# The rows of maxima transposed at unit 26 of a stage, right behind a weighing, in place of unit 24, between two weighings

## Chip, cores and metric

One core of one Trainium2 chip runs the whole program. The metric is the device time of one execution in microseconds; the program before takes 2254.86 us (median of 3 runs, 2253.78 to 2256.43).

## What is computed

16 images of 128 channels and 1024 tokens go through multi-head attention and then through a mixture of experts. Cut to what matters here:

```python
q, k, v = (einsum('btc,hcd->bhtd', xs, W) for W in (Wq, Wk, Wv))     # 8 heads of size 16
att = softmax(einsum('bhtd,bhsd->bhts', q, k) / 4, axis=-1)           # 1024 x 1024 for each head
out = einsum('bhts,bhsd->bhtd', att, v)
x = x + (out.transpose(0, 2, 1, 3).reshape(B, T, -1) @ Wproj + bproj)
t = tokens(x); t = t + top2_mixture_of_experts(layernorm(t))          # 16 experts, hidden 512
```

The softmax subtracts each row's maximum before the exponential. The change is in the attention phase, in the way those maxima reach the second product.

## The kernel before

**Stages and units.** Heads are done in two groups (G = 2) of four, and the 1024 queries in two halves, so an image has 4 stages; a stage has UNITS = 32 units, one for each of 8 blocks of keys and 4 heads. An image has SLOTS = 128 units, numbered u = 0 to 127 below; "unit 90" of image 7 is unit 26 of its stage 2. The order is written out by hand: on every engine a Python function `batch` runs over the 128 units and emits what belongs to each, so each engine's instructions stand in one fixed order and wait for each other by semaphores.

**What a unit does.** TensorE issues one maxima matmul (`max_unit`, L1531), which runs LEAD = 45 units ahead, and one score matmul (`score_unit`, L1555). VectorE takes the row maximum of the first (`take_max`, L1009); four banks of PSUM (MRING = 4) lie between them, so that TensorE is at most four ahead. ScalarE takes the exponential of the second (`exp_unit`, L848). After every fourth unit or so TensorE weighs values with four finished exponentials (`weigh`, L1572; its four matmuls stand as x8 in the profile); within a stage this is behind units 2, 7, 10, 14, 18, 22, 26 and 30. 

**Front banks.** Scores, projections and all transposes share three banks (FRONT = 3), which go round in the order of issue; the fourth of such results must wait until ScalarE has emptied the bank of the first. `FRONT_BANK` follows this order from `front_order`, where "m" stands at unit MSLOT of a stage.

**The rows of maxima.** At unit 19 of a stage VectorE has all maxima of the next stage, and it splits them into two parts by unit 21. At unit MSLOT TensorE transposes them (`rows_of_maxima`, L1541, four matmuls), ScalarE copies the result to `m_row` (`copy_m`, L882), and two DMAs on SP's queue (`load_m`, L414, 8 KB) put them beside the queries in `arena_b`. The first score of the next stage waits for these DMAs (`m_loaded`). The transposes behind unit 24 of stage s = 0, 1, 2, 3 belong to stage s + 1, or to stage 0 of the next image.

**SP's queue** is in order too. In each image it holds, among others, the moves of stacked queries and keys for a later stage (`stack`, L405, 12 DMAs of 64 KB each for a group and a layer). The last three moves of two such sets stand right behind a `load_m`:

```python
stack(b, 1, 1, every[:9], at + 15)
load_m(b, 1)
stack(b, 1, 1, every[9:], at + 26)
...
stack(b + 1, 0, 1, every[:9], at + 78)
load_m(b, 3)
if not last:
    stack(b + 1, 0, 1, every[9:], at + 90)
```

The first set is waited for by the maxima matmul that stands at unit 35 (`stacked[1][1]`, maximum number 80), the second by the one at unit 99 (`stacked[0][1]` of the next image, number 144 = 99 + 45).

Of the kernel before, what the change touches and what calls it, by code (L numbers as in the profile page):

```python
# [25 lines left out]
UNITS = TB * HG  # L26
SLOTS = STAGES * UNITS
LEAD = 45
MSLOT = 24
FRONT, MRING = 3, 4  # L30
PRING = 16
NORMS = 14
# [70 lines left out]
def front_order():  # L103
# [5 lines left out]
    for b in range(B):  # L109
        for u in range(SLOTS):  # L110
# [5 lines left out]
            if b > 0:  # L116
# [4 lines left out]
                if u == COUNT_AT:  # L121
                    yield "counts", b - 1, 0
            if u % UNITS == MSLOT and not (b == B - 1 and u > 96):
                yield ("m", b, u // UNITS + 1) if u // UNITS + 1 < STAGES else ("m", b + 1, 0)
# [11 lines left out]
def metaformer(nc, x, wq, wk, wv, wproj, bproj, wgate, w1, w2, out):  # L136
    ctx = ExitStack()
    with ctx:
# [703 lines left out]
        def _(act):  # L842
# [34 lines left out]
            def copy_m(b, s):  # L877

                k = STAGES * b + s
                wait(act, m_psum, k + 1)  # L880
                wait(act, m_loaded, 16 * SIDES * k)
                nc.scalar.activation(m_row[0:MROWS, :], front("m", *divmod(k, STAGES))[0:MROWS, :], ACT.Copy).then_inc(m_copied, 1)  # L882
# [18 lines left out]
            def copy_rows(b, half):  # L901
                wait(act, rows_normed, TB * (b + 1))
                wait(act, scattered, 256 * b)
                js = slice(4 * half, 4 * half + 4)
                nc.scalar.activation(rows[:, 1, js, 0:C], rows[:, 0, js, 0:C], ACT.Copy).then_inc(rows_copied, 1)
# [14 lines left out]
            def batch(b, first, last):  # L920
                for u in range(SLOTS):
# [8 lines left out]
                    if not first:  # L930
# [8 lines left out]
                        if u in ROWS_AT:  # L939
                            copy_rows(b - 1, ROWS_AT.index(u))  # L940
                    if u % UNITS == MSLOT and not (last and u > 96):
                        copy_m(b, u // UNITS + 1)
# [542 lines left out]
        def _(pe):  # L1485
# [50 lines left out]
            def rows_of_maxima(b, s):  # L1536
                k = STAGES * b + s
                to = take_front("m", *divmod(k, STAGES), m_copied, k + 1)
                wait(pe, m_split, 2 * (k + 1))
                for t in range(4):  # L1540
                    last = nc.tensor.transpose(to[0:MROWS, t * P:(t + 1) * P],  # L1541
                                               m_parts_f[:, t, :, :, :].rearrange("p s a l -> p (s a l)"), ident[:, :])
                last.then_inc(m_psum, 1)
# [58 lines left out]
            def count_tokens(b):  # L1602

                w = 3 * E
                to = take_front("counts", b, 0, cs_taken, b + 1)
                wait(pe, masks_ready, b + 1)
                nc.tensor.matmul(to[:, 0:TB * w], tri_b[:, :], masks_b[:, :, :], start=True, stop=False)
                for d in range(1, TB):
                    nc.tensor.matmul(to[:, d * w:TB * w], ones_b[:, :], masks_b[:, 0:TB - d, :], start=False,
                                     stop=(d == TB - 1))  # L1610
                for j in range(TB):
                    last = nc.tensor.matmul(to[:, TB * w:(TB + 1) * w], ones_b[:, :], masks_b[:, j, :],
                                            start=(j == 0), stop=(j == TB - 1))
                last.then_inc(cs_psum, 1)
# [18 lines left out]
            def batch(b, first, last):  # L1633
                for u in range(SLOTS):
# [15 lines left out]
                    if not first:  # L1650
# [6 lines left out]
                        if u == COUNT_AT:  # L1657
                            count_tokens(b - 1)
                    if u % UNITS == MSLOT and not (last and u > 96):
                        rows_of_maxima(b, u // UNITS + 1)  # L1660
# [110 lines left out]
```

## Time and profile before

| what | value |
|---|---|
| median of 3 runs | 2254.86 us |
| the profiled execution: its time, its span | 2254.34 us, 2252.5 us |
| TensorE matmuls busy | 2106.4 us (94%) |
| VectorE busy | 1841.2 us (82%) |
| ScalarE busy | 1528.6 us (68%) |
| one image in the steady part of the attention phase | about 100.8 us (units of 0.79 us) |
| first and last transposes of the rows of maxima | 56.34 us and 1635.82 us |

The attention phase lasts until about 1660 us, then the experts follow. Time outside the span (2254.34 less 2252.5, 1.8 us) is start and end of the program. An idle time in brackets in a row of the timeline stands for the engine just before the row's first instruction, with what ended it. A row merges equal instructions that follow each other closely; its length reaches from the first start to the last end. Matmuls are pipelined, so what counts is the distance between starts.

### The profile page before, as it was taken

The page shows a single profiled execution, that of the slowest core. Times are in us where ns is not written, and L with a number is a line of the kernel's source. Part 1 is how long each engine was busy: PE and PEld are TensorE (multiplying, and loading weights), DVE is VectorE, ACT ScalarE, POOL GpSimd, SP SyncE. Part 2 cuts the span into 40 slices and gives each one's busy share as a digit, 9 for nine tenths or more (in the row PEclk, how much of TensorE's full clock was granted, in tenths as well). Part 3 has the DMA queues.
Part 4 walks back from the last instruction along what each step waited for, and adds up shares of the span by engine and source line. Part 5 has one row for each costly group of instructions (what it writes and reads, how often), then busy time and mean ns, then how long its engine had stood idle before and what let it go on. Part 6 is the DMA issues. An engine that isn't in the chain of part 4 may idle for free. (4 is left out here: it accounts for less than half of the span.)

```text
span 2252.5 us, 53329 instructions
## 1 busy us (share of the span) xinstructions
PE 2106.4 (94%) x16914; PEld 1175.1 (52%) x16914; DVE 1841.2 (82%) x4370; ACT 1528.6 (68%) x3169; POOL 1048.7 (47%) x1650
## 2 busy tenths in 40 slices
PE   5999999999999999999999999999969999899996
PEld 2333333334333333334333333333339999899996
DVE  6899999999999999999999999999925445345664
ACT  1777777777777777777777777777646566466552
POOL 3204454454445455454445455444246577455542
PEclk7999999999999999999999999999989999999997
DMA  5223323132323323232323323223162223222586
GB/s 127 48 44 63 60 58 76 36 71 45 69 53 72 61 53 74 37 70 51 67 52 68 71 43 74 39 60 57 40 190 70 71 71 86 78 71 71 159 253 178
DMA packets 135695, 171.09 MB, mean 76 GB/s; under 512 B 31568, under 2 KB 101592, under 8 KB 135414
## 3 DMA queue, kind: packets, MB, share of 16 engines
q1 hardware_dynamic: 118582, 134.25, 27.9%
q0 software_dynamic: 16896, 34.12, 4.3%
q8 instruction: 115, 1.88, 0.3%
q14 instruction: 102, 0.84, 0.1%
HBM read 64.86 MB, written 48.87 MB: 50 GB/s over the span
## 5 line engine op out<-in xcount | busy, mean ns | idle before, releaser
L1009 DVE TENSOR_REDUCE sb_m_red<-banks 128x1 f32<-128x512 f32 x2048 | 1318.8, 678 | 85.6 <-PE banks L1531 79.7
L848 ACT ACTIVATE sb_arena_a<-banks 128x512 f32<-128x512 f32 x2048 | 1088.7, 600 | 329.4 <-PE banks L1555 325.7
L1555 PE MATMUL banks<-sb_arena_b 64*128 64x512 f32 x2048 | 788.7, 460 | 21.5 <-DVE sb_res L1068 9.6
L1531 PE MATMUL banks<-sb_arena_b 62*128 62x512 f32 x2048 | 741.9, 448 | 40.4 <-DVE sb_m_red L1009 27.4
L1531 PEld LDWEIGHTS banks<-sb_arena_b 62*128 62x128 f32 x2048 | 340.7, 188 | 571.7 <-DVE sb_m_red L1009 468.5
L1572 PE MATMUL banks<-sb_arena_a,sb_arena_d 128*32 128x512 f32 x4096 | 546.0, 605 | 11.0 <-DVE sb_o_t L1041 9.3
L777 POOL DMA_INDIRECT sorted_rows<-sb_rows,sb_place x256 | 250.8, 980 | 343.3 <-PE banks L1555 325.4
L1555 PEld LDWEIGHTS banks<-sb_arena_b 64*128 64x128 f32 x2048 | 331.6, 185 | 139.5 <-ACT sb_arena_a L848 95.5
L821 POOL DMA_INDIRECT expert_out<-sb_arena_d x272 | 271.6, 999 | 242.6 <-DVE sb_arena_d L1401 178.1
L1685 PE MATMUL banks<-sb_arena_d,sb_arena_c 128*128 128x128 f32 x2176 | 290.4, 277 | 1.2 <-ACT sb_arena_d L954 0.7
L1694 PE MATMUL banks<-sb_arena_c 128*128 128x128 f32 x2176 | 289.0, 276 | 0.0
L1394 DVE COPY sb_arena_c<-sb_arena_b 128x512 f32 x272 | 134.9, 496 | 168.3 <-PE banks L1694 163.4
L1685 PEld LDWEIGHTS banks<-sb_arena_d,sb_arena_c 128*128 128x128 f32 x2176 | 267.1, 193 | 1.8 <-ACT sb_arena_d L954 1.8
L1694 PEld LDWEIGHTS banks<-sb_arena_c 128*128 128x128 f32 x2176 | 266.5, 193 | 0.0
L961 ACT ACTIVATE sb_arena_c<-banks 128x512 f32<-128x512 f32 x272 | 162.4, 597 | 113.8 <-PE banks L1685 112.2
L1391 DVE COPY sb_arena_c<-sb_arena_a 128x512 f32 x272 | 116.6, 429 | 80.2 <-issue 46.6
L968 ACT ACTIVATE sb_arena_d<-banks,sb_arena_d 128x128 f32<-128x128 f32 x272 | 99.9, 367 | 99.2 <-PE banks L1694 92.8
L1572 PEld LDWEIGHTS banks<-sb_arena_a,sb_arena_d 128*32 128x32 f32 x4096 | 80.6, 108 | 154.1 <-issue 93.8
L657 POOL TENSOR_SCALAR sb_arena_d<-sb_v_st 128x512 f32<-128x512 f32 x32 | 19.6, 614 | 269.0 <-ACT sb_v_st L873 207.7
L954 ACT ACTIVATE sb_arena_d<-banks 128x128 f32<-128x128 f32 x272 | 73.4, 270 | 35.7 <-PE banks L1677 35.2
L1677 PE MATMUL banks<-sb_ident,sb_arena_d 128*128 128x128 f32 x272 | 74.8, 276 | 19.3 <-DMA sb_arena_d<-sorted_rows 19.3
L1510 PE MATMUL banks<-sb_xt,sb_wq_r 128*128 128x512 f32 x128 | 74.2, 667 | 7.9 <-POOL sb_xt L639 7.7
(167 smaller groups left out, 1597.4 us busy)
## 6 DMA issues: line engine op xcount, KB each, us to landing
sb_arena_b<-sb_arena_c SPq DMA_DIRECT2D x768, 64.0 KB, 2.3
sb_arena_d<-sorted_rows SPq DMA_DIRECT2D x272, 66.0 KB
sb_x_in<-in_x_dram SPq DMA_DIRECT2D x16, 512.0 KB, 3.9
sb_res<-in_x_dram SPq DMA_DIRECT2D x16, 512.0 KB, 3.6
sb_x_all<-sb_res SPq DMA_DIRECT2D x16, 512.0 KB, 3.1
expert_out<-sb_arena_d POOLq DMA_INDIRECT x272
sorted_rows<-sb_rows,sb_place POOLq DMA_INDIRECT x256
sb_arena_a<-in_L_ffn_w_dram SPq DMA_DIRECT2D x4, 1024.0 KB, 7.4
```

The source lines that it names most:

```text
L777: nc.gpsimd.indirect_dma_start(out=sorted_rows[:, :], out_offset=bass.IndirectOffsetOnAxis(ap=place[:, k, j:j + 1], axis=0), in_=rows[:, k ...
L821: nc.gpsimd.indirect_dma_start(out=expert_out[:, :], out_offset=bass.IndirectOffsetOnAxis(ap=blk_dest[:, s % WR:s % WR + 1], axis=0), in_= ...
L848: nc.scalar.activation(probs[:, u % PRING, :], front("score", b, u), ACT.Exp, scale=SCALE).then_inc(exp_done, 1)
L961: nc.scalar.activation(hid[:, s % 2, :], ps_h[:, s % 2, :], ACT.Relu).then_inc(hid_done, 1)
L1009: nc.vector.tensor_reduce(out=m_red[:, s % 2, at:at + 1], in_=ps_max[:, m % MRING, :], axis=AX.X, op=ALU.max).then_inc(max_taken, 1)
L1391: nc.vector.tensor_copy(w1_blk[:, s % WR, :], w1_all[:, bass.ds(e, 1), :].rearrange("p a h -> p (a h)")).then_inc(w1_copied, 1)
L1394: nc.vector.tensor_copy(w2_blk[:, s % WR, :], w2_all[:, bass.ds(e, 1), :, :].rearrange("p a c d -> p (a c d)")).then_inc(w2_copied, 1)
L1531: nc.tensor.matmul(ps_max[:, m % MRING, :], qs[rows_of, g, l, half * HALF + t * P:half * HALF + (t + 1) * P], ks[rows_of, g, l, kh * HALF: ...
L1555: nc.tensor.matmul(to, ks[rows_of, g, l, i * P:(i + 1) * P], qs[rows_of, g, l, half * HALF:(half + 1) * HALF], start=True, stop=True).then ...
L1572: last = nc.tensor.matmul(ps_pv[32 * h:32 * h + 32, :], v_pad[:, i, HG * g + h, :], probs[:, (4 * n + h) % PRING, :], start=(i == 0), stop ...
L1685: last = nc.tensor.matmul(ps_h[:, s % 2, c * P:(c + 1) * P], w1_blk[:, s % WR, c * P:(c + 1) * P], blk_xt[:, s % 2, :], start=True, stop=True)
L1694: last = nc.tensor.matmul(ps_o[s % WR], hid[:, s % 2, c * P:(c + 1) * P], w2_blk[:, s % WR, c * P:(c + 1) * P], start=(c == 0), stop=(c == ...
```

## The change

One constant. `front_order` and the `batch` functions of TensorE and ScalarE read it; VectorE, GpSimd and SP keep their order.

```diff
-MSLOT = 24
+MSLOT = 26
```

On TensorE the four transposes (L1541) stood behind the score of unit 24, in the midst of the four units between the weighing behind unit 22 and that behind unit 26. This is the place in stage 1 of an image; before:

```order
L1572 MATMUL banks<-sb_arena_a,sb_arena_d 32x512 x4
L1531 MATMUL banks<-sb_arena_b 128x512
L1555 MATMUL banks<-sb_arena_b 128x512
L1531 MATMUL banks<-sb_arena_b 128x512
L1555 MATMUL banks<-sb_arena_b 128x512
L1541 MATMUL banks<-sb_ident,sb_m_parts 8x128 x4
L1531 MATMUL banks<-sb_arena_b 128x512
L1555 MATMUL banks<-sb_arena_b 128x512
L1531 MATMUL banks<-sb_arena_b 128x512
L1555 MATMUL banks<-sb_arena_b 128x512
L1572 MATMUL banks<-sb_arena_a,sb_arena_d 32x512 x4
L1531 MATMUL banks<-sb_arena_b 128x512
```

The same stretch of TensorE's program in the changed kernel:

```order
L1572 MATMUL banks<-sb_arena_a,sb_arena_d 32x512 x4
L1531 MATMUL banks<-sb_arena_b 128x512
L1555 MATMUL banks<-sb_arena_b 128x512
L1531 MATMUL banks<-sb_arena_b 128x512
L1555 MATMUL banks<-sb_arena_b 128x512
L1531 MATMUL banks<-sb_arena_b 128x512
L1555 MATMUL banks<-sb_arena_b 128x512
L1531 MATMUL banks<-sb_arena_b 128x512
L1555 MATMUL banks<-sb_arena_b 128x512
L1572 MATMUL banks<-sb_arena_a,sb_arena_d 32x512 x4
L1541 MATMUL banks<-sb_ident,sb_m_parts 8x128 x4
L1531 MATMUL banks<-sb_arena_b 128x512
```

The transposes have moved past two units and one weighing; everything else keeps its place.

On ScalarE the copy (L882) moves past two exponentials (L848). Before, in the same stage:

```order
L848 ACTIVATE sb_arena_a<-banks 128x512 x8
L882 ACTIVATE sb_m_row<-banks 8x512
L848 ACTIVATE sb_arena_a<-banks 128x512 x6
L873 ACTIVATE sb_v_st<-banks 128x512
```

And in the changed kernel:

```order
L848 ACTIVATE sb_arena_a<-banks 128x512 x10
L882 ACTIVATE sb_m_row<-banks 8x512
L848 ACTIVATE sb_arena_a<-banks 128x512 x4
L873 ACTIVATE sb_v_st<-banks 128x512
```

SP's queue is the same in both. This is its stretch from the moves between stages 1 and 2 to the end of an image; the three moves (L405 x3) stand between two loads of rows of maxima (L414):

```order
L405 DMA sb_arena_b<-sb_arena_c 16x1024 x21
L414 DMA sb_arena_b<-sb_m_row 2x2x512 x2
L405 DMA sb_arena_b<-sb_arena_c 16x1024 x3
L414 DMA sb_arena_b<-sb_m_row 2x2x512 x2
L405 DMA sb_arena_b<-sb_arena_c 16x1024 x12
```

Since nothing in it moves, the three moves follow the load in front of them, whenever its copy is done.

## Rows read from the trace of the kernel before

**Rows 1.** Busy time of each engine, mean over nine windows of 102 us
```profile
sum 918.00, PE 874.98 PEld 354.43 DVE 874.97 ACT 692.75 POOL 422.92; mean PE 97.22 PEld 39.38 DVE 97.22 ACT 76.97 POOL 46.99
```

**Rows 2.** Timeline of TensorE, image 7, units 87 to 99
```profile
831.07 1.07 PE L1572 MATMUL banks<-sb_arena_a,sb_arena_d 128*32 128x512 f32 x8
...
832.73 0.60 PE L1541 MATMUL banks<-sb_ident,sb_m_parts 128*8 128x128 f32 x4
...
834.20 1.06 PE L1572 MATMUL banks<-sb_arena_a,sb_arena_d 128*32 128x512 f32 x8
835.20 0.50 PE L1531 MATMUL banks<-sb_arena_b 62*128 62x512 f32 x1
...
836.41 0.49 PE L1555 MATMUL banks<-sb_arena_b 64*128 64x512 f32 x1
836.83 1.06 PE L1572 MATMUL banks<-sb_arena_a,sb_arena_d 128*32 128x512 f32 x8
...
838.17 0.63 PE L1531 MATMUL banks<-sb_arena_b 62*128 62x512 f32 x2
...
839.05 0.50 PE L1555 MATMUL banks<-sb_arena_b 64*128 64x512 f32 x1
839.48 1.06 PE L1572 MATMUL banks<-sb_arena_a,sb_arena_d 128*32 128x512 f32 x8
840.47 0.49 PE L1531 MATMUL banks<-sb_arena_b 62*128 62x512 f32 x1
```

**Rows 3.** Timeline of ScalarE, the same stretch
```profile
832.63 1.09 ACT L848 ACTIVATE sb_arena_a<-banks 128x512 f32<-128x512 f32 x2 [0.57 <-PE banks L1555]
833.60 0.57 ACT L882 ACTIVATE sb_m_row<-banks 8x512 f32<-8x512 f32 x1
...
835.76 2.07 ACT L848 ACTIVATE sb_arena_a<-banks 128x512 f32<-128x512 f32 x4 [0.64 <-PE banks L1555]
838.40 2.06 ACT L848 ACTIVATE sb_arena_a<-banks 128x512 f32<-128x512 f32 x4 [0.57 <-PE banks L1555]
```

**Rows 4.** Timeline of VectorE, the same stretch
```profile
835.73 5.12 DVE L1009 TENSOR_REDUCE sb_m_red<-banks 128x1 f32<-128x512 f32 x8 [0.64 <-PE banks L1531]
841.00 1.29 DVE L1009 TENSOR_REDUCE sb_m_red<-banks 128x1 f32<-128x512 f32 x2 [0.16 <-PE banks L1531]
```

**Rows 5.** Timeline of SP's queue, the same stretch
```profile
834.20 1.36 SPq L414 DMA_DIRECT2D sb_arena_b<-sb_m_row  x2
835.66 1.84 SPq L405 DMA_DIRECT2D sb_arena_b<-sb_arena_c  x3
```

**Rows 6.** Timeline of TensorE, ScalarE: a projection behind a weighing, unit 62
```profile
813.06 1.06 PE L1517 MATMUL banks<-sb_wv_sb,sb_xt 128*32 128x128 f32 x32
...
814.19 0.60 ACT L873 ACTIVATE sb_v_st<-banks 128x512 f32<-128x512 f32 x1 [1.02 <-PE banks L1517]
```

**Rows 7.** Timeline around unit 32 of image 10: ScalarE, SP, TensorE
```profile
1084.49 0.57 ACT L882 ACTIVATE sb_m_row<-banks 8x512 f32<-8x512 f32 x1
...
1087.32 1.36 SPq L414 DMA_DIRECT2D sb_arena_b<-sb_m_row  x2
...
1090.01 0.50 PE L1555 MATMUL banks<-sb_arena_b 64*128 64x512 f32 x2 [0.52 <-DMA sb_arena_b<-sb_m_row]
```

**Rows 8.** DMA issues: size in KB, median us from issue to landing
```profile
sb_arena_b<-sb_arena_c SPq DMA_DIRECT2D x768, 64.0 KB, 2.3
```

**Rows 9.** Timeline around unit 0 of image 7: ScalarE, TensorE
```profile
759.85 1.58 ACT L848 ACTIVATE sb_arena_a<-banks 128x512 f32<-128x512 f32 x3 [0.57 <-PE banks L1555]
...
761.09 0.50 PE L1555 MATMUL banks<-sb_arena_b 64*128 64x512 f32 x1
```

**Rows 10.** Timeline around unit 32 of image 2: ScalarE, SP, TensorE
```profile
278.47 0.57 ACT L882 ACTIVATE sb_m_row<-banks 8x512 f32<-8x512 f32 x1
...
280.47 1.47 SPq L414 DMA_DIRECT2D sb_arena_b<-sb_m_row  x2
...
283.99 0.50 PE L1555 MATMUL banks<-sb_arena_b 64*128 64x512 f32 x2 [0.54 <-DMA sb_arena_b<-sb_m_row]
```

## The prediction

> **What bounds the kernel now.** I read the busy times of the attention phase first, then the timeline of one image unit by unit on TensorE, ScalarE, VectorE and SP's queue. Over nine windows of 102 us TensorE and VectorE are both busy for 97.22 us [rows 1]: neither hides behind the other, and they take turns. The turns show in the idle times of VectorE. In the stretch of units 87 to 99 it runs dry twice, 0.64 us before 835.73 and 0.16 us before 841.00, each time until TensorE's first maxima matmul behind a weighing [rows 4]. There TensorE decides, and a delay of TensorE goes straight into the time.
>
> TensorE's own pace between two weighings is set by ScalarE and the three front banks. From 834.20 to 836.83 and on to 839.48 a group of four units and a weighing takes 2.63 and 2.65 us [rows 2]. The first unit of a group starts at 835.20, its exponential at 835.76 and lasts about 0.60 [rows 3]; the fourth score needs its bank and starts at 836.41, 0.05 behind the exponential's end at 836.36; the weighing follows 0.42 later and takes 1.00 until the next unit [rows 2]. With the transposes in its midst the group from 831.07 to 834.20 takes 3.13 us: in the old place they cost 0.50.
>
> Second, the chain behind the transposes: transposes 832.73 [rows 2], copy 833.60 to 834.17 [rows 3], the two loads from 834.20, three moves of stacked rows from 835.66 to 837.50 [rows 5]. How long the loads take to be seen is read where TensorE waits for them, in image 10: issued at 1087.32, the score starts at 1090.01, 2.69 later [rows 7]. In the stretch of rows 2 this would be 836.89, and the score of unit 96 starts at 838.17, so there is 1.28 us of slack. The third move has one move's length of 0.54 (an estimate: 1.84 for three, less 0.65 from start to start twice) and starts at 836.96; with 2.3 to land [rows 8] it is there at 839.26, and the maxima matmul of unit 99, which needs it, starts at 840.47 [rows 2]: 1.21 us of slack. The change spends both.
>
> **The change part by part.** Nothing is added or removed: 63 times four transposes of 0.60 us, a copy of 0.57 and the waits of two DMAs move; on SP's queue, what stands behind those DMAs moves with them.
>
> *The new place.* Units 89 and 90 lose the transposes ahead of them. The score of unit 90 needs the bank of unit 87, whose exponential starts at 832.63 and ends at 833.23 [rows 3]; so the score starts at 833.28, the weighing at 833.70, and the transposes at 834.70. That is 1.97 later than now.
>
> *The copy.* The trace has a case of work with a front bank right behind a weighing, the projection of unit 62: it ends at 814.12 and its copy starts at 814.19 [rows 6], since ScalarE has caught up during the weighing. So the copy starts 0.67 behind the start of the transposes, where it now starts 0.87 behind: 835.37, end 835.94, against 834.17 now. The load chain is 1.77 later, not 1.97.
>
> *TensorE behind it.* The transposes hold TensorE for 0.53; unit 91 starts at 835.23. Its exponential comes behind the copy, 0.48 after the copy's start (833.60, next start 834.08 by the pitch of four exponentials in 2.06 us [rows 3]), so 835.85 to 836.45; unit 94's score at 836.50, the weighing at 836.92 instead of 836.83. The group costs 0.09 more than in the old place. Where VectorE is behind (stage 1, whose choosing of experts keeps it busy), this shows only at unit 67. I count 0.09 for 16 stages of that kind: **1.4 us**.
>
> *The first score of the next stage.* Stage 2 to 3: natural start 838.26, loads seen at 835.94 + 0.03 + 2.69 = 838.66, so TensorE stands still for 0.40. It is nearly absorbed: the score of unit 98 has to wait for the exponential of unit 95, and starts at 839.05, although TensorE could be there at about 838.65 (838.17 and two steps of 0.24: two maxima matmuls in 0.63, one of them 0.40 long) [rows 2]. The same for stage 3 to stage 0 of the next image, but there a transpose of x stands behind unit 1 and uses up that reserve: unit 2's score starts at 761.09 [rows 9], and the exponential of unit 0, late by 0.49, pushes it. Unit 31's score starts 0.56 ahead of the first exponential at 759.85 [rows 9], unit 0's 0.34 behind that, at 759.63; with the 0.49 it is 760.12, its exponential runs from 760.68 to 761.28 (now it starts at 760.34), and unit 2's score starts at 761.33, 0.24 late. VectorE is dry at unit 3 there, so this counts: 15 images by 0.24 = **3.6 us**. Bounds: 0.09 each if all is absorbed (1.4 us), 0.49 each if nothing is (7.4 us).
>
> *Stage 0 to 1.* Here SP decides already: in image 10 the copy ends at 1085.06, yet the load is issued at 1087.32, behind nine moves, and TensorE waits for it [rows 7]. A copy 1.77 later ends at 1086.83: still in time. In image 2 the copy ends at 279.04 and the load is issued at 280.47 [rows 10]; with the new copy it is 280.84, 0.37 late. Eight images (1 to 6, 8, 9) are like image 2. There the landing is slow (3.52 from issue to score [rows 10] against 2.69), which may mean that the DMA queue decides and not the issue: 0 to 0.37 each, I take half: **1.5 us**. What is queued behind, three moves, has over 1 us of slack.
>
> *The moves behind the load of stage 3.* The largest term. SP waits for the copy with the three moves for the next image behind it. Load at 835.97, third move 2.76 later at 838.73, landing 841.03. TensorE would be at unit 99 at 840.47 + 0.09 = 840.56; it now starts at about 841.07, 0.60 later than before. VectorE is dry at that point (idle until 841.00 [rows 4]) and then has the four steps of dividing in units 100 to 103, so it decides what follows and carries the 0.60 along. 15 images by 0.60 = **9.0 us**. Bounds: 0.16 less each if VectorE's present idle time covers that much (6.6), and 1.77 - 1.21 + the 0.40 of unit 96 if the two waits added up (0.96 each, 14.4).
>
> The Trainium skill, "DMA: Bandwidth & Descriptors", section on the anatomy of one DMA, gives about 2.0 us plus the bytes over 436 GB/s, a fit for DMAs issued from GpSimd; for 64 KB that is an estimate of 2.15 us where rows 8 have 2.3. By it the term of the moves would be 0.15 less for each image, 6.8 us in place of 9.0.
>
> Sum: 1.4 + 3.6 + 1.5 + 9.0 = 15.5 us. Against the profiled execution's 2254.34 us that is **2269.8 us**; that execution lies 0.5 below the median of the runs shown, which changes nothing here.
>
> **The rivals.**
> - *The late loads and moves are hidden.* For it: each wait is seen behind a weighing or an exponential that TensorE waits for anyway. Against: at unit 99 VectorE has nothing left, and nothing behind it has reserve. Then only the 0.09 of the group is left, at 63 places: 5.7 us, **2260 us**.
> - *No change at all.* VectorE's stock of four maxima would have to cover all of it. It is dry behind the transposes now [rows 4], which speaks against it. **2254.9 us.**
> - *The DMAs are slower when they come together.* Image 2 shows 3.52 from issue to score where image 10 has 2.69 [rows 7, 10]. If the shifted loads met such a queue, 0.83 would be added at unit 99 of 15 images and at unit 0 as well: 25 us more, **2294 us**. Against: in stage 3's place SP issues the load 0.03 behind the copy's end [rows 3, 5], so it has been waiting and its earlier moves have had time to drain, while in image 2 it comes straight from nine moves.
> - *Faster.* The transposes fall into a hole. Behind a weighing TensorE waits for the exponential of the group's first unit, the 0.40 between 838.65 and 839.05 above. If the transposes, put ahead of the group, took only what that wait leaves, they would cost 0.53 - 0.40 = 0.13 and not 0.50. That gives 0.37 in some 32 stages in which TensorE decides, 12 us: **2243 us**. It decides only if the loads are then seen within about 2.5 us of the copy's start (838.26 less 0.40, less 835.37); they take 0.57 + 0.03 + 2.69 = 3.29. Against: the wait begins with the group's first score, so whatever stands ahead of that score delays both.
>
> **How the numbers follow.** The forecast, slower by the sum of waits, has a chance of 0.80; hidden waits 0.07; no change 0.05; slower DMAs 0.04; faster 0.04. The bounds of its terms add up to 1.4 + 1.4 + 0 + 6.6 = 9 us and 1.4 + 7.4 + 3.0 + 14.4 = 26 us; hardly all at one end, so I take the range from 2261 to 2279, which also nearly takes in the hidden waits. About 0.2% (4.5 us) is what a measurement can tell from no change: slower by more than that 0.88 (forecast, slower DMAs, part of the hidden case), within it 0.08, faster 0.04.
>
> **What would show it.** In the profile after: copies (L882) that start about 0.67 behind the transposes; TensorE idle at the first score of stages 0 and 3, ended by the DMA from `m_row`, some 0.4 us each, and at a maxima matmul (L1531) ended by the DMA from `arena_c`, about 0.5 us in each of 15 images (now in hardly any); VectorE idle about 0.7 us before unit 99. An image should take about 101.8 us where it takes 100.8. The prediction is wrong if unit 99 starts without a wait, or if the groups with transposes take less than 3.1 us and no wait appears behind them.

## The result, and the profile after

The changed kernel takes 2270.59 us (median of 4 runs, 2267.79 to 2271.32), the kernel before 2254.94 in the same comparison: a ratio of 1.0064, 95% interval 1.0052 to 1.0076. It is slower by 15.7 us; 15.5 were forecast, on top of the profiled execution's time: 2269.8 us. The changed kernel's profiled execution is one of 2270.59 us, with a span of 2268.7.

Busy time of each engine, mean over the nine windows of [rows 1]:

```profile
sum 918.00, PE 872.62 PEld 358.58 DVE 865.69 ACT 688.60 POOL 418.98; mean PE 96.96 PEld 39.84 DVE 96.19 ACT 76.51 POOL 46.55
```

VectorE, which was busy as long as TensorE, has lost one microsecond in each window of 102: it waits for TensorE more often. The place is image 7 again, units 91 to 99. TensorE's timeline, to be held against [rows 2]:

```profile
842.63 1.06 PE L1572 MATMUL banks<-sb_arena_a,sb_arena_d 128*32 128x512 f32 x8
843.63 0.60 PE L1541 MATMUL banks<-sb_ident,sb_m_parts 128*8 128x128 f32 x4
844.16 0.50 PE L1531 MATMUL banks<-sb_arena_b 62*128 62x512 f32 x1
...
845.38 0.50 PE L1555 MATMUL banks<-sb_arena_b 64*128 64x512 f32 x1
845.81 1.07 PE L1572 MATMUL banks<-sb_arena_a,sb_arena_d 128*32 128x512 f32 x8
...
847.15 0.40 PE L1531 MATMUL banks<-sb_arena_b 62*128 62x512 f32 x1
847.55 0.51 PE L1555 MATMUL banks<-sb_arena_b 64*128 64x512 f32 x2
...
848.45 1.06 PE L1572 MATMUL banks<-sb_arena_a,sb_arena_d 128*32 128x512 f32 x8
849.97 0.50 PE L1531 MATMUL banks<-sb_arena_b 62*128 62x512 f32 x1 [0.46 <-DMA sb_arena_b<-sb_arena_c]
```

ScalarE, for [rows 3]:

```profile
844.27 0.59 ACT L882 ACTIVATE sb_m_row<-banks 8x512 f32<-8x512 f32 x1 [0.65 <-PE banks L1541]
844.76 2.03 ACT L848 ACTIVATE sb_arena_a<-banks 128x512 f32<-128x512 f32 x4
```

VectorE, for [rows 4]:

```profile
844.69 2.48 DVE L1009 TENSOR_REDUCE sb_m_red<-banks 128x1 f32<-128x512 f32 x4 [0.68 <-PE banks L1531]
847.34 2.48 DVE L1009 TENSOR_REDUCE sb_m_red<-banks 128x1 f32<-128x512 f32 x4 [0.16 <-PE banks L1531]
850.51 1.29 DVE L1009 TENSOR_REDUCE sb_m_red<-banks 128x1 f32<-128x512 f32 x2 [0.69 <-PE banks L1531]
```

SP's queue, for [rows 5]:

```profile
844.88 1.36 SPq L414 DMA_DIRECT2D sb_arena_b<-sb_m_row  x2
846.35 1.83 SPq L405 DMA_DIRECT2D sb_arena_b<-sb_arena_c  x3
```

Read in order: the copy starts 0.64 behind the transposes (0.87 before), so ScalarE was indeed free. The loads go 0.02 behind the copy's end, and the score of unit 96 starts at 847.55, 2.67 behind their issue; its maxima matmul had started at 847.15, so TensorE stood still for 0.40 where the two used to start together. That wait is absorbed: the weighing follows the one before by 2.64. Then comes the dear one. The weighing from 848.45 is followed by the next maxima matmul 1.52 later, not 1.00, and the row names what ended the wait: the DMA from `arena_c`, the third of the moves that SP could issue only behind the late load. VectorE, dry for 0.16 there before, is dry for 0.69.

The groups' own price: from weighing 26 to weighing 30 with the transposes 3.18, and a plain group is 2.64; in [rows 2] it was 3.13 and 2.63. The new place costs 0.05 more.

The view of waits of TensorE's weight loads and ScalarE, attention phase (total us, times, longest) shows the new waits over all images:

```profile
PEld banks L1555 <- DMA sb_arena_b<-sb_m_row: 28.7, 47, 1.4
PEld banks L1531 <- DMA sb_arena_b<-sb_arena_c: 24.5, 19, 1.7
```

Before, the first was 13.2 us in 15 waits (all at unit 32) and the second 4.8 us in 5. A weight load has waits that cost nothing, so these are counts of places and no sum of losses.

At unit 0 of image 8 the same wait is not absorbed. TensorE, for [rows 9]:

```profile
869.93 0.40 PE L1531 MATMUL banks<-sb_arena_b 62*128 62x512 f32 x1
870.32 0.50 PE L1555 MATMUL banks<-sb_arena_b 64*128 64x512 f32 x2
870.65 0.40 PE L1531 MATMUL banks<-sb_arena_b 62*128 62x512 f32 x1
870.98 0.66 PE L1502 MATMUL banks<-sb_ident,sb_x_in 128*128 128x128 f32 x4
871.57 0.49 PE L1531 MATMUL banks<-sb_arena_b 62*128 62x512 f32 x1
```

The score waits 0.39, and the transposes of x and unit 2 follow without a hole in which the delay could vanish.

To see where an image loses its time over the whole phase, the start of each maxima matmul after was set against that of the same matmul before, both counted from unit 0 of the image, and averaged over images 1 to 13. What this gives at unit (us late, cumulated):

```
unit            3     27    33    60    92    99    124   128
changed kernel  0.18  0.22  0.33  0.37  0.42  0.96  1.00  1.01
```

So an image is 1.01 us longer. Steps: 0.18 at the head (the wait at unit 0), 0.04 or 0.05 behind the transposes of each stage (27, 60, 92, 124), 0.11 at units 32 and 33, and 0.53 at unit 99. All but one are nearly the same in every image (the head 0.16 to 0.23, the groups 0.03 to 0.06, unit 99 0.46 to 0.53 and once 0.83). The step at unit 33 is not: it runs from -0.16 to 0.34 over the images, and in the trace of run 2 below, which changes nothing there, its mean is 0.08. The 0.11 is therefore not told from the scatter of one trace.

### The profile page after: what moved, and what is told of

Same layout as the page of the kernel before. It is cut to its first block and busy times, and to the rows that moved or that the text cites. A ratio compares the mean times of both kernels' runs of the same rounds, so it can differ in the third digit from the quotient of the medians.

```text
span 2268.7 us, 53329 instructions
## 1 busy us (share of the span) xinstructions
PE 2118.4 (93%) x16914; PEld 1187.0 (52%) x16914; DVE 1842.0 (81%) x4370; ACT 1534.5 (68%) x3169; POOL 1048.2 (46%) x1650
## 5 line engine op out<-in xcount | busy, mean ns | idle before, releaser
L848 ACT ACTIVATE sb_arena_a<-banks 128x512 f32<-128x512 f32 x2048 | 1085.4, 600 | 297.1 <-PE banks L1555 290.0
L882 ACT ACTIVATE sb_m_row<-banks 8x512 f32<-8x512 f32 x64 | 37.6, 587 | 70.3 <-PE banks L1541 70.3
```

Source lines behind the costliest of these rows:

```text
L848: nc.scalar.activation(probs[:, u % PRING, :], front("score", b, u), ACT.Exp, scale=SCALE).then_inc(exp_done, 1)
```

## Experiments

Times are medians, ratios are against the kernel before on the same chip with their 95% intervals. "Late at unit" is the measure above.

### 1. Unit 26, moves ahead of the late load

```diff
-                    stack(b + 1, 0, 1, every[:9], at + 78)
+                    stack(b + 1, 0, 1, every, at + 78)
                 load_m(b, 3)
                 if not last:
-                    stack(b + 1, 0, 1, every[9:], at + 90)
                     load_m(b, 4)
```

> The changed kernel (unit 26), but on SP's queue the last three moves of the set for the next image's stage 0 stand ahead of the load of stage 3's rows of maxima, not behind it. Late moves (my account): the wait of the maxima matmul at unit 99 is gone, 0.48 to 0.53 us in each of 15 images, some 7.5 us less than the changed kernel, about 2263 us, and the waits at units 0 and 96 stay. Rival, the place behind the weighing itself costs the time: no change against the changed kernel, about 2270 us.

2261.03 us, ratio 1.0026 (1.0015 to 1.0037). The changed kernel's ratio is 1.0064, so the edit takes off 0.38% or 8.6 us (9.6 between the two medians, which were taken beside different runs of the kernel before). SP's queue in this kernel:

```profile
832.22 6.97 SPq L405 DMA_DIRECT2D sb_arena_b<-sb_arena_c  x10
840.84 1.36 SPq L414 DMA_DIRECT2D sb_arena_b<-sb_m_row  x2
```

The row of moves is the last ten of the twelve; all are out 1.6 us before the load. TensorE (lines here are one lower):

```profile
844.41 1.07 PE L1571 MATMUL banks<-sb_arena_a,sb_arena_d 128*32 128x512 f32 x8
845.41 0.49 PE L1530 MATMUL banks<-sb_arena_b 62*128 62x512 f32 x1
```

Unit 99 follows its weighing by 1.00 without a wait. The step at unit 99 falls from 0.53 to 0.01 and an image is 0.48 us longer, not 1.01. The largest term is shown, the rival (the place itself) falls. The head of the image is also 0.09 cheaper than in the changed kernel, since the wait of the score at unit 0 is 0.31 and not 0.40: from the loads' issue to that score it is 2.58 us and not 2.67. Runs 11 and 12, which have the same order of SP's queue here, show 2.58 as well, and run 7, which has the old order, 2.67. So it goes with the order; why was not found.

### 2. The control: unit 24, moves ahead of the load

The same edit with MSLOT = 24.

> The kernel before (unit 24) with the same reordering of SP's queue as in the first run: the control. Late moves: the three moves had 1.2 us of slack at unit 99, so nothing changes, 2255 us within 2. Rival, the reordering is worth 7 us wherever the transposes stand: about 2247 us.

2255.27 us, ratio 0.9998 (0.9989 to 1.0007): no change, as expected. Its trace, of the slowest of its executions (2259.43 us), has images that are 0.17 us longer, none of it at units 0 and 99; so much can one trace differ without the kernel's time having changed. With its 1.2 us of slack the order of the queue was worth nothing; it is the lateness that makes it count.

### 3. Unit 25

```diff
-MSLOT = 24
+MSLOT = 25
```

> Transposes at unit 25, one unit from the old place, still ahead of the weighing. Late chain: the copy on ScalarE starts 0.49 us later than before (one exponential more ahead of it), which stays below the 1.2 us of slack at units 96, 0 and 99: no wait appears, 2255 us within 2. Rival, the time grows with each unit that the transposes are later: half of the whole change, about 2263 us.

2258.09 us, ratio 1.0013 (1.0004 to 1.0022). Not half of the change, but not nothing either: 1 us outside what I expected. In the trace no wait appears at units 0, 96 or 99 (unit 99 is no later than unit 96, and the scores of units 0 and 96 start with their maxima matmuls); an image is 0.15 us longer, in steps of 0.04 or 0.05 behind each stage's transposes, of which the first is made good again at unit 33, where SP's queue decides when stage 1 may start. My expectation had left out that the group with the transposes gets dearer one unit further on, too.

### 4. Unit 26, but ahead of the weighing

On TensorE `rows_of_maxima` is called before `weigh` at that unit; the banks and ScalarE's order are those of the changed kernel.

> Transposes at unit 26 as in the changed kernel, with the same order of banks and the same place of the copy on ScalarE, but ahead of the weighing of that unit. Late chain: the transposes start about 1.0 us earlier than in the changed kernel, the copy 0.8 us earlier, some 1.0 later than before, within the slack of 1.2: hardly a wait, 2255 to 2258 us. Rival, unit 26 as such costs the time (banks, ScalarE's order): about 2270 us.

2261.09 us, ratio 1.0022 (1.0012 to 1.0031). Two thirds of the loss are gone, but 3 us more are left than I had expected. TensorE:

```profile
834.97 0.60 PE L1541 MATMUL banks<-sb_ident,sb_m_parts 128*8 128x128 f32 x4
835.50 1.06 PE L1572 MATMUL banks<-sb_arena_a,sb_arena_d 128*32 128x512 f32 x8
...
838.15 1.07 PE L1572 MATMUL banks<-sb_arena_a,sb_arena_d 128*32 128x512 f32 x8
```

Late at unit 3: 0.00, at unit 99: 0.14 with no step there. So no late load and no late move costs anything. What is left is the group: 0.10 behind each stage's transposes where it is 0.04 or 0.05 behind a weighing. The four steps of 0.10 come to 0.40 an image, but 0.17 are made good at unit 33, in the same way as in run 3, so that an image is 0.25 longer. The place behind the weighing is thus the cheaper one for the transposes themselves, and still the worse one for the kernel, because it is 1.0 us later.

### 5. Unit 28: the slack is spent

```diff
-MSLOT = 24
+MSLOT = 28
```

> Transposes two units later still, at unit 28, between two weighings like the old place. Late chain: the slack is spent, so what the copy is later (0.87 us against the changed kernel, two exponentials stand ahead of it) adds in full at unit 99, at unit 0 and at unit 32, and 0.4 us at unit 64, 3.0 us for each of 15 images: about 2315 us. Rival, only the place behind a weighing is bad and the lateness is not: between 2255 and 2262 us.

2315.59 us, ratio 1.0268 (1.0253 to 1.0284), against 2315 expected. TensorE, image 8:

```profile
868.65 0.51 PE L1555 MATMUL banks<-sb_arena_b 64*128 64x512 f32 x2 [0.93 <-DMA sb_arena_b<-sb_m_row]
...
869.55 1.06 PE L1572 MATMUL banks<-sb_arena_a,sb_arena_d 128*32 128x512 f32 x8
871.70 0.50 PE L1531 MATMUL banks<-sb_arena_b 62*128 62x512 f32 x1 [1.08 <-DMA sb_arena_b<-sb_arena_c]
```

Both waits of the changed kernel are here. The scores of units 0 and 96 wait 1.33 us behind their maxima matmuls, 0.93 more than in the changed kernel, which is about what the copy is later. The step at unit 99 is 1.45 in its least image, also 0.92 more than 0.53, but 1.82 on average: SP issues the third move 2.76 us behind the load as before, yet in run 5 it takes 2.28 to 2.91 us to land, where it took 2.21 to 2.28 in the changed kernel. Why it lands later was not looked for. At unit 64 the score waits 0.48, and that is absorbed, so the 0.4 that I had counted there did not come. One unit to 25 costs 2.4 us, two units to 26 cost 15.7, four to 28 cost 60: a price with a threshold, which is what slack looks like, and not one in proportion. An image is 4.4 us longer where I had expected 1.0 and 3.0 more, from a sum that was too high at unit 64 and too low at unit 99: that the total came within 1 us is in part luck.

### 6 and 7. The transpose of x out of the reserve's way

```diff
-XT_AT, QK_AT, V_AT = (1, 5), (33, 41, 44, 48), (62, 66)
+XT_AT, QK_AT, V_AT = (3, 5), (33, 41, 44, 48), (62, 66)
```

with MSLOT = 24 and with MSLOT = 26, one execution each.

> The kernel before (unit 24) with the first transpose of x at unit 3 of an image, not at unit 1: the control for the next run. 2255 us within 5; no wait at unit 0.

> The changed kernel (unit 26) with the first transpose of x at unit 3. Reserve theory: the wait of the first score of an image stays at 0.4 us, but it is absorbed by unit 3 as that of unit 96 is, so against the run before the maxima matmuls are late by under 0.05 us at unit 3, not by 0.18. Rival, the transpose of x has no part in it: 0.18 late at unit 3 as in the changed kernel. Time 2.5 us lower than the changed kernel if the reserve is right.

2254.21 and 2264.94 us. Between these two, maxima matmuls are late by 0.01 at unit 3 and by 0.51 more from unit 96 to unit 99, though the first score of the image still waits 0.41 behind its maxima matmul. So with nothing behind unit 1 the wait is absorbed like that at unit 96, and the price at unit 0 in the changed kernel comes from the transpose of x, which uses the same hole. The time is 5.65 us below the changed kernel's, where 2.5 were expected; the traces give 0.12 an image, 1.8 us, and the rest can't be told from the spread of single executions. That an image of the first run is 0.25 us shorter than before was not looked for; its single time does not tell it from no change.

### 8. Can the old wait at unit 32 be taken away? First try

Unit 24, with the load of stage 1 ahead of the seventh move:

```diff
-                stack(b, 1, 1, every[:9], at + 15)
+                stack(b, 1, 1, every[:6], at + 15)
                 load_m(b, 1)
-                stack(b, 1, 1, every[9:], at + 26)
+                stack(b, 1, 1, every[6:], at + 21)
```

> The kernel before (unit 24), but on SP's queue the load of stage 1's rows of maxima stands ahead of the seventh move of the set around it, not behind the ninth. If SP's queue is what makes the first score of stage 1 late (unit 32, in every image after the first), the load is issued right behind its copy, the wait is gone, and unit 35 comes 0.6 us earlier in 15 images: about 2246 us. Rival, the landing is what takes long, behind the moves' own 64 KB each: 2252 us or no change.

2254.67 us, ratio 0.9998 (0.9989 to 1.0007). A miss, and the rival's reason is not the right one either: the wait at unit 32 is gone, and unit 33 is 0.92 us earlier. But TensorE has a new one at unit 35:

```profile
788.32 1.12 PE L1510 MATMUL banks<-sb_xt,sb_wq_r 128*128 128x512 f32 x2 [0.25 <-ACT sb_arena_a L848]
...
791.53 0.50 PE L1531 MATMUL banks<-sb_arena_b 62*128 62x512 f32 x1 [0.66 <-DMA sb_arena_b<-sb_arena_c]
```

and ScalarE one at its copy behind unit 33, which may overwrite the parts only when all moves have landed:

```profile
791.59 0.60 ACT L867 ACTIVATE sb_arena_c<-banks 128x512 f32<-128x512 f32 x1 [2.35 <-DMA sb_arena_b<-sb_arena_c]
```

The six moves behind the load end later, since SP now stands still until the copy is done. It is the changed kernel's mechanism once more: work behind a wait in an ordered queue.

### 9 and 10. Second try: fill SP's idle time

```diff
                 stack(b, 1, 0, every, at + 1)
+                stack(b, 1, 1, every[:3], at + 15)
                 if not first:
                     store_x1(b - 1)
-                stack(b, 1, 1, every[:9], at + 15)
+                stack(b, 1, 1, every[3:9], at + 18)
```

> The kernel before (unit 24), but the first three moves of the set for stage 2's second layer stand ahead of the store of the image's x1 on SP's queue, where SP stands idle for some 9 us until that store may go. Then the load of stage 1's rows of maxima is issued right behind its copy (the wait at unit 32 goes) and the last three moves are not later than now (no new wait at unit 35, which took the gain in the run with the early load): 0.6 us for each of 15 images, about 2246 us. Rival, VectorE takes over as the bound there, or the landing is what takes long: 2252 us or no change.

2236.46 us, ratio 0.9910 (0.9895 to 0.9925), 20 us faster, twice what I had expected. SP's queue:

```profile
772.30 0.52 SPq L421 DMA_DIRECT2D sb_x_all<-sb_res  x1
772.91 3.90 SPq L405 DMA_DIRECT2D sb_arena_b<-sb_arena_c  x6
777.32 1.38 SPq L414 DMA_DIRECT2D sb_arena_b<-sb_m_row  x2
778.80 2.77 SPq L405 DMA_DIRECT2D sb_arena_b<-sb_arena_c  x3
```

The load now goes 5.0 us and six moves behind the store, where it went 6.4 to 7.3 us and nine moves behind it, and no first score waits any more. An image is 0.90 us shorter in the trace, 0.60 of it at units 32 to 35, as expected, and 0.33 between units 45 and 55.

I had not expected those 0.33, but the trace shows where they come from. They are not the same in every image: six of the images 1 to 13 gain 0.70 there, the others nothing, and it hangs on which of two engines starts first. VectorE's step L1120 in the choosing of experts meets a step of GpSimd (L651). Image 4:

```profile
495.80 1.42 POOL L651 TENSOR_TENSOR sb_arena_c<-sb_arena_c 128x512 fp32r<-128x512 f32 x1
495.81 0.28 DVE L1120 TENSOR_TENSOR sb_gat<-sb_tmp,sb_small 128x128 f32<-128x128 f32 x1
```

Image 5, and TensorE's wait at unit 54 there:

```profile
595.23 1.28 POOL L651 TENSOR_TENSOR sb_arena_c<-sb_arena_c 128x512 fp32r<-128x512 f32 x1
595.26 1.40 DVE L1120 TENSOR_TENSOR sb_gat<-sb_tmp,sb_small 128x128 f32<-128x128 f32 x1
600.42 0.50 PE L1532 MATMUL banks<-sb_arena_b 62*128 62x512 f32 x1 [0.88 <-DVE sb_m_red L1010]
```

Started up to 0.02 us behind GpSimd's step, VectorE's takes 0.28; started 0.03 or more behind it, it ends only 0.15 behind the end of GpSimd's. In the images that gain, this step is 1.1 us shorter, and the wait of 0.88 at unit 54 is gone. In the kernel before GpSimd's step is 0.09 us or more ahead in every image, and none gains; in run 9 the earlier stage 1 has brought the two starts together. So of the 20 us some 9 (0.60 in 15 images) are SP's, and part of the rest is a coincidence of two engines. The profiled execution was the slowest of its four (2243.44 us); whether the faster ones win this race in more images, no trace shows.

The same with the transpose of x at unit 3:

> The same with the first transpose of x at unit 3, which in its own run took 0.25 us off an image: the two add, about 2242 us. Rival, the one takes the place of the other: 2246 us.

2236.90 us, ratio 0.9912 (0.9896 to 0.9927): in the time the one doesn't add to the other. (In its trace five of the images 1 to 13 gain the 0.70.) Both beat the kernel before and the changed kernel; run 9 is the simpler one.

### 11 and 12. Unit 26 with its price taken away

Run 10 with MSLOT = 26 and the moves of run 1:

> Transposes at unit 26 as in the changed kernel, with everything that made its lateness cost taken away: moves ahead of stage 3's load, transpose of x at unit 3, three moves ahead of the store. Late chain: against the run at unit 24 with the same relief only the dearer groups (0.05 us each in 63 places) and a rest of wait at unit 32 are left, 3 to 6 us, about 2247 us, below the kernel before. Rival, something else of the change costs time: above 2255 us.

2254.70 us, ratio 0.9991 (0.9982 to 1.0000): 8 us above what I expected. The view of waits has the reason:

```profile
ACT sb_arena_c L867 <- DMA sb_arena_b<-sb_arena_c: 16.3, 14, 2.3
PEld banks L1531 <- DMA sb_arena_b<-sb_arena_c: 14.8, 15, 1.6
```

I had moved the moves only from behind stage 3's load. Behind stage 1's, three still stood, and with SP's queue no longer late there the late copy became what they wait for. So they were put ahead too:

```diff
-                stack(b, 1, 1, every[3:9], at + 18)
+                stack(b, 1, 1, every[3:], at + 18)
                 load_m(b, 1)
-                stack(b, 1, 1, every[9:], at + 26)
```

> The run before (unit 26, relieved) with the one set of moves that still stood behind a late load put ahead of it: the last three moves of the set around stage 1's load, which that run's trace shows landing late for the copy behind unit 33 (2.3 us of ScalarE's wait) and for unit 35. Late chain: then only the dearer groups are left (0.05 us in 63 places, 3 us) and the waits of first scores, some 0.4 us each, of which part is absorbed (at unit 32 some 0.25 for each of 15 images): 2240 to 2246 us. Rival, something in the change that I have not named costs the rest: 2250 us or more.

2264.48 us, ratio 1.0032 (1.0020 to 1.0043). The waits for moves are gone, and the kernel is slower still. SP's queue and then TensorE:

```profile
781.33 6.15 SPq L405 DMA_DIRECT2D sb_arena_b<-sb_arena_c  x9
787.53 1.35 SPq L414 DMA_DIRECT2D sb_arena_b<-sb_m_row  x2
788.92 0.40 SPq L386 DMA_DIRECT2D sb_x_in<-in_x_dram  x1
```

```profile
790.77 0.50 PE L1554 MATMUL banks<-sb_arena_b 64*128 64x512 f32 x2 [0.61 <-DMA sb_arena_b<-sb_m_row]
```

From the load's issue to the score it is 3.24 us here. Over images 1 to 14 this time is 2.67 to 2.75 in run 11, where SP stood idle before the load, and 2.69 to 4.20, mean 3.29, in run 12, where the load comes straight behind nine moves (and has 512 KB of x behind it). In the kernel before, also behind nine moves, it is 3.15 on average. The kernel before, whose load has three moves and not x behind it, is nearly as slow, which speaks for the nine moves ahead as the cause and not for x; but they don't slow every image, since the least values there are 2.69 too. Neither of these two orders of SP's queue brings the price of unit 26 down to the groups alone: in one the moves wait for the load, in the other the load lands late behind the moves. Others, with some of the moves ahead, were not tried. Against run 10, 17.8 us (run 11) and 27.6 us (run 12) are lost. On average over the images the step at unit 33 is 0.54 and 1.23, of which 0.36 and 0.92 are left at unit 35; 0.27 and 0.34 more go between units 45 and 55, where the gain of VectorE's race with GpSimd is gone.

## Why the prediction was right

**Which engine decides, and where.** Right. VectorE's idle time grew by what TensorE lost where it counted (0.16 to 0.69 before unit 99). Not each wait is in the time: the 0.40 at unit 96 is absorbed, as forecast.

**The new place.** Forecast: transposes 1.97 later, copy 0.67 behind their start, load chain 1.77 later, group 0.09 dearer. Measured: copy 0.64 behind, group 0.05 dearer. Term: 1.4 us for 16 stages at 0.09, and 0.09 inside the terms at units 0 and 99; in fact 0.04 or 0.05 in each of the four stages of an image, about 2.8 us for 63 places. The place was right and its size for one group twice what was measured. That stage 1, where VectorE is behind, would show it only at unit 67 was wrong: it shows at unit 60, with 0.05, like the others. That ScalarE's copy ahead of the exponential is the reason was worked out and no run tests it alone.

**The first score of the next stage.** Forecast: a wait of 0.40, absorbed at unit 96 and not at unit 0, where it costs 0.24. Measured: 0.40 at both, absorbed at unit 96; at unit 0 an image loses 0.18 there and 0.04 in the group before it. Runs 6 and 7 show why.

**Stage 1.** Forecast 0 to 0.37 in 8 images, half taken, 0.10 for each image; measured 0.11 at unit 33 besides the group's 0.04, with the scatter said above, so that this agreement is partly luck. That SP's nine moves already made this stage late, and so hid most of the change, is shown from the other side by runs 10 and 11: with SP relieved, the same change costs 0.54 at unit 33, and 0.36 are left at unit 35.

**The moves behind the load of stage 3.** Forecast 0.60 at unit 99 with the group in it, 9.0 us; measured 0.53 and 0.05, and run 1 takes 8.6 us off by moving three DMAs (some 1.4 of it at unit 0). Run 2 shows that this holds only beyond the slack. With the group, as in the forecast, 0.58 in 15 images is 8.7 us. By the figure of the Trainium skill ("DMA: Bandwidth & Descriptors", anatomy of one DMA) the term would have been 6.8 us. The third move behind the load, which is the one that counts, landed 2.21 to 2.28 us behind its issue: a little less than the 2.3 of [rows 8], and more than the 2.15 that the prediction estimated from that figure.

**The sum.** Measured in the trace, an image is 1.01 us longer, 15.2 us in 15 images, against 15.5 forecast and 15.7 in the medians. The terms are less exact than the sum: unit 0 cost 0.22 with its group where 0.24 were forecast, unit 99 0.58 for 0.60, and the group by itself half of its price, but in all four stages.

**The rivals.** "Hidden" and "no change" fell with the wait at unit 99. "Slower DMAs" did not happen in the changed kernel at stages 3 and 0, where SP is idle ahead of the load: from issue to score it is 2.65 to 2.72 us in images 1 to 14. Run 12 made the condition at stage 1 and the effect came, 0.6 us on average where 0.83 had been priced. "Faster" fell since the transposes delay the whole group behind them.

Where I misjudged things was in the experiments: the group's price in runs 3 and 4, the waits at units 64 and 99 in run 5, the moves behind the load in runs 8 and 11, VectorE's part of the gain in run 9, and the landing in run 12.

## What to carry to other kernels

Before moving an operation later, follow its result to the in-order queue that waits for it, and list what stands behind that wait: here three unrelated DMAs cost more than everything that needed the result. Measure the slack of each of these consumers; below it a shift costs little, beyond it every part counts in full. And where a queue idles in front of a wait, put work ahead of that wait that is already ready: here SP stood idle for some 8.5 us ahead of a store, three moves put there made the kernel 20 us faster, and about 9 of these are SP's own. When a gain is larger than forecast, look at it image by image before trusting it.

## What the runs showed of the hardware

A pair of 8 KB DMAs from SP is seen by TensorE 2.67 to 2.75 us after the first one's issue at stage 1 of run 11, where SP was idle before (2.58 at unit 0 of runs 1, 11 and 12), and 2.69 to 4.20, mean 3.29, in run 12, where nine 64 KB moves were issued right ahead of it, though SP's issue itself is no longer (1.35 against 1.37 us for the two).

Transposes directly behind a weighing are cheaper than ones directly ahead of it (0.04 or 0.05 against 0.10 us on the group). ScalarE's copy starts 0.64 us behind the transposes' start there, after an idle time of 0.65, and 0.78 in run 4, right behind an exponential; that this makes the difference was not tested.

A `tensor_tensor` of VectorE with both inputs in SBUF (128 x 128, 0.28 us alone) that starts 0.03 us or more behind GpSimd's `tensor_tensor` of 128 x 512 (1.28 us) ends 0.15 us after it, up to 1.40 us long; where it starts 0.01 or 0.02 behind, it keeps its 0.28 and GpSimd's takes 1.42 to 1.44 (runs 9 and 10, stage 1 of images 1 to 14).
